# A fused decoder layer on one core: output weights staged elsewhere, start loads reordered, last mixing on VectorE, and a new order of all steps

## The reference

```python
x = x + attn(layernorm(x), wq, wk, wv, wo)           # (4, 512, 256), 16 heads, keys of 16, values of 64
x = x + xattn(ctx, ctx, layernorm(x), fm_w, fm_b, fc_w, fc_b)
x = x + ffn(layernorm(x), W_r, W_k, W_v, mu_r, mu_k)
# attn: softmax over the query axis of q.k / 4, times v, then the output projection
# xattn: features exp(z), exp(-z) of queries and of 64 context rows, softmax over the 64, then fc
# ffn: xr = prev + mu_r (x - prev), xk = prev + mu_k (x - prev);  out = sigmoid(xr W_r) * (relu(xk W_k)^2 W_v)
```

## Time and profile before

| | |
|---|---|
| median of 3 executions | 449.89 us (449.42 to 451.17) |
| the profiled execution | 449.9 us |
| its span | 448.1 us |
| instructions | 8243 |
| TensorE clock granted, mean | 1.00 |

### The profile page before, as it was taken

The page is one execution under the profiler, slowest core; times in us unless marked ns, Lnnn a source line. Parts: engine busy times, 40 slices in busy tenths (PEclk is TensorE's granted clock), DMA queues, the critical chain, the costliest instruction groups (busy, mean ns, idle before and its releaser), DMA issues.

```text
span 448.1 us, 8243 instructions
## 1 busy us (share of the span) xinstructions
PE 426.5 (95%) x2738; PEld 274.4 (61%) x2738; DVE 367.7 (82%) x668; ACT 300.9 (67%) x760; POOL 161.2 (36%) x206
## 2 busy tenths in 40 slices
PE   6999999999989999999999999999999999879896
PEld 4745454466545865566655785576555674467775
DVE  4688877798998887888999978798999888669762
ACT  3687988676796666666778566666787757529521
POOL 2163203117232513427052622427331533534442
PEclk9999999999999999999999999999999999999999
DMA  7668302435210015145103002642003100000001
GB/s 241 234 236 269 142 1 96 143 107 197 75 47 1 1 55 179 64 150 187 45 6 119 0 2 103 197 153 91 0 1 111 57 1 1 23 2 1 1 25 47
DMA packets 22561, 38.23 MB, mean 85 GB/s; under 512 B 2808, under 2 KB 7160, under 8 KB 22392
## 3 DMA queue, kind: packets, MB, share of 16 engines
q1 hardware_dynamic: 22520, 37.71, 24.6%
HBM read 23.02 MB, written 14.68 MB: 84 GB/s over the span
## 4 chain that ended last, share of the span: by engine, by line
PE 75%; DVE 9%; ACT 8%; issue 4%; DMA 1%; POOL 1%; SPq 0%; POOLq 0%; ACTq 0%; DVEq 0%
PE av_bank L909 22%; PE m_bank L841 9%; PE s_pair L895 8%; PE m_bank L845 6%; DVE nmax L1355 4%; ACT e_sb L1148 3%; PE m_bank L1045 3%; PE m_bank L961 2%; PE m_bank L1057 2%; PE m_bank L982 2%; PE m_bank L1117 2%; PE m_bank L1106 2%; PE m_bank L926 2%; PE m_bank L1073 2%; PE m_bank L945 1%
## 5 line engine op out<-in xcount | busy, mean ns | idle before, releaser
L1148 ACT ACTIVATE e_sb<-s_pair,nmax 128x512 f32<-128x512 f32 x256 | 174.1, 692 | 62.0 <-DVE nmax L1355 61.8
L1355 DVE TENSOR_REDUCE nmax<-s_pair 128x2 f32<-128x1024 f32 x128 | 152.4, 1213 | 21.5 <-PE s_pair L895 20.6
L909 PE MATMUL av_bank<-e_sb,v_sb 128*64 128x512 f32 x512 | 120.1, 602 | 1.0 <-POOL v_sb L1627 0.8
L1627 POOL TENSOR_TENSOR v_sb<-v_sb,rsum 128x256 f32<-128x256 f32 x64 | 39.7, 622 | 156.6 <-DVE rsum L1363 156.6
L909 PEld LDWEIGHTS av_bank<-e_sb,v_sb 128*64 128x64 f32 x512 | 32.6, 136 | 62.8 <-issue 53.2
L895 PE MATMUL s_pair<-q_st,k_st 64*128 64x512 f32 x256 | 49.9, 456 | 4.8 <-ACT e_sb L1148 4.8
L1148 ACT ACTIVATION_READ_ACCUMULATOR e_sb<-s_pair,nmax 128x1 f32 x256 | 53.6, 209 | 0.0
L895 PEld LDWEIGHTS s_pair<-q_st,k_st 64*128 64x128 f32 x256 | 21.3, 184 | 39.1 <-ACT e_sb L1148 25.2
L841 PE MATMUL m_bank<-wo_hi,ot_hi 128*128 128x256 f32 x128 | 36.4, 290 | 0.0
L845 PE MATMUL m_bank<-wo_lo,ot_hi 128*128 128x256 f32 x128 | 35.0, 279 | 0.0
L1654 POOL TENSOR_TENSOR sx<-sx,xrec 128x512 f32<-128x512 f32 x24 | 24.8, 1045 | 26.9 <-DVE xrec L1541 26.9
(11 more groups left out here) (186 smaller groups left out, 830.9 us busy)
## 6 DMA issues: line engine op xcount, KB each, us to landing
q_st<-q_parts SPq DMA_DIRECT2D x31, 256.0 KB, 3.8
k_st<-k_parts SPq DMA_DIRECT2D x31, 256.0 KB, 3.8
k_parts<-qkt_hi SPq DMA_DIRECT2D x7, 512.0 KB, 3.1
k_parts<-qkt_lo SPq DMA_DIRECT2D x7, 512.0 KB, 4.1
q_parts<-qkt_hi SPq DMA_DIRECT2D x8, 256.0 KB, 2.0
q_parts<-qkt_lo SPq DMA_DIRECT2D x8, 256.0 KB, 2.3
out<-x_sb SPq DMA_DIRECT2D x8, 256.0 KB, 2.2
x_sb<-in_x SPq DMA_DIRECT2D x3, 512.0 KB, 5.0
```

Source lines behind the costliest of these rows:

```text
L909: mm = pe.matmul(av_bank[n % AV_BANKS][64 * par:64 * par + 64, :], v_sb[:, m, 2 * p + par, :], e_sb[:, (4 * q + 2 * i + par) % E_RING, :], ...
L1148: act.activation(e_sb[:, g % E_RING, :], s_pair[k // 2][:, k % 2, :], ACT.Exp, bias=nmax[:, g % 8:g % 8 + 1], accum_out=esum[:, q % 4, k:k ...
L1355: dve.tensor_reduce(nmax[:, at:at + 2], s_pair[i][:, :, :], AX_X, ALU.max, negate=True)\
L1627: pool.tensor_tensor(v_sb[:, m:m + 2, 2 * p:2 * p + 2, :], v_sb[:, m:m + 2, 2 * p:2 * p + 2, :], rsum[:, q % 4, :].rearrange("p (m h) -> p ...
```

## The change

1. The output weights are staged in `sx`, the tile of the cross scores; the value projections lose their wait for them, and the first write of `sx` (`xs`, DVE) gains one.
2. SP loads the query/key weights second, right behind x; the output weights follow the value weights at once, and the feature loads move behind `ld 3`, the `fc` weights behind `ld 7` of sequence 0.
3. In `xs` and `pv` on PE the waits for what was done long ago come first; odd `xs` steps drop the wait for `z`.
4. The output projection of the last half-set of heads is split in two steps, `op` and `op_last`.
5. For sequence 3 `mix_r` is finished on DVE by two SCALAR_TENSOR_TENSOR instructions (`mix_rec`) instead of three on POOL.
6. All places are new. ACT at the start: `cut v1` from place 21 to 4, both `t1` before `cut first`; DVE: `t1 (0)` before `cut qk`, `qk (1, 0)` before the first `max`; POOL: `cut v1` from place 5 to 3. PE keeps the first twelve steps, then swaps `v (0, 2)` and `qk (1, 0)`. In the middle most steps move by a few places. Around attention step 22 `t2 (1)` goes four places up on PE, and on ACT `v`, `xs` and `pt` copies go behind the four `exp` of step 21; on ACT `t1 (0)` of sequence 1 goes behind `exp [5, 3]`. At the end: DVE's `fv 2 (0)` goes from before `ot_lo 31` to between `ln2_do (1)` and `t2 (1)`; POOL's `mix 2 (1)` goes behind both `ln2`; on PE `xs (1)` goes before `z (1)` and on ACT `z (1)` before `xs (0)`; the two `warm` steps after `fr 3 (0)` and the four after `fv 3 (0)`, and the one between the last `fk` and `fr`, are elsewhere: PE has `fr 3 (0)`, `t3 (1)`, `fv 3 (0)`, `fk 3 (1)`, `fr 3 (1)`, `fv 3 (1)` in a row, and seven `warm` steps behind them.

The lines of the diff outside the tables (of the tables a few stand for the rest):

```diff
-    ("cut", 0, ("v1",), dict(act=21, pool=5)),
+    ("cut", 0, ("v1",), dict(act=4, pool=3)),
-    ("load", 0, ("feat",), dict(sp=0)),
-    ("load", 0, ("o",), dict(sp=1)),
+    ("load", 0, ("feat",), dict(sp=8)),
+    ("load", 0, ("o",), dict(sp=0)),
...
-        wo_raw = v_sb[:, :, H // 2:, :].rearrange("p t h v -> p t (h v)")
+        wo_raw = sx
...
-                if before or unit[1] == B - 1:
+                if before or unit[1]:
                     eng.wait_ge(exp_ready, TILES)
...
+            sp.dma_start(wqk_raw, wqk).then_inc(wqk_in, 16)
             sp.dma_start(id_sb[:], ident).then_inc(id_in, 16)
             sp.dma_start(first_raw, wfirst).then_inc(first_in, 16)
-            sp.dma_start(wqk_raw, wqk).then_inc(wqk_in, 16)
...
-                for p in range(4):
-                    if p == 3:
-                        pe.wait_ge(ot_hi_ready, b * NP + 4 * hh + 4)
+                for p in range(3):
...
+                if (b, hh) != (B - 1, 1):
+                    op_last(b, hh, tt)
+            def op_last(b, hh, tt):
+                unit = ("op", b, (hh, tt))
+                pe.wait_ge(ot_hi_ready, b * NP + 4 * hh + 4)
...
             def xs(b, t):
+                if t == 0:
+                    pe.wait_ge(kblk_ready, b + 1)
                 for unit in units:
                     wait_bank(pe, unit)
-                for r in range(2):
-                    wait_emptied(pe, ("z", b, (t // 2, r)))
-                if t == 0:
-                    pe.wait_ge(kblk_ready, b + 1)
+                if t % 2 == 0:
+                    for r in range(2):
+                        wait_emptied(pe, ("z", b, (t // 2, r)))
...
             def fr(b, half):
-                pe.wait_ge(mixr_ready, 2 * b + half + 1)
+                if b == B - 1:
+                    pe.wait_ge(mixr_last, half + 1)
+                else:
+                    pe.wait_ge(mixr_ready, 2 * b + half + 1)
...
-                    if b == 0 and hh:
-                        act.wait_ge(cut_lo["o"], 1)
...
-                    if b == 0 and hh:
-                        dve.wait_ge(cut_lo["o"], 1)
...
                 link(dve.tensor_reduce(xmax[:, n % 4, :], src, AX_X, ALU.max, negate=True))
+                if n == 0:
+                    dve.wait_ge(cut_lo["o"], 1)
...
+            def mix_rec(b, half):
+                dve.wait_ge(mixk_ready, 2 * b + half + 1)
+                prev = xt3[:, :, half * HALF:(half + 1) * HALF]
+                for c in range(DC):
+                    ins = dve.scalar_tensor_tensor(out=mix_r[:, c, :], in0=mix_r[:, c, :], scalar=mu_sb[:, 0, c:c + 1],
+                                                   in1=prev[:, c, :], op0=ALU.mult, op1=ALU.add)
+                ins.then_inc(mixr_last, 1)
```

More of the change, by code:

```diff
@@ L130 @@
[L130 to L139, removed]
+    ("warm", 0, (3, 1), dict(pe=341)),
@@ L485 @@
[L485 to L486 removed]
+    dict(scores=14, weigh=21, max=(14, 15), exp=(13, 14, 15, 16), rsum=19, scale=4),
+    dict(scores=17, weigh=22, max=(17, 18), exp=(18, 19, 20, 21), rsum=21, scale=5, ot_hi=30, ot_lo=29),
+    dict(scores=20, weigh=28, max=(22, 23), exp=(23, 24, 25, 26), rsum=30, scale=7),
+    dict(scores=23, weigh=29, max=(26, 27), exp=(27, 28, 31, 32), rsum=31, scale=8, ot_hi=38, ot_lo=37),
@@ new lines @@
+    dict(scores=66, weigh=75, max=(87, 88), exp=(97, 98, 99, 100), rsum=96, scale=23),
+    dict(scores=69, weigh=80, max=(91, 93), exp=(103, 105, 106, 107), rsum=97, scale=26, ot_hi=120, ot_lo=110),
+    dict(scores=72, weigh=84, max=(98, 100), exp=(109, 110, 111, 112), rsum=107, scale=27),
+    dict(scores=76, weigh=85, max=(104, 105), exp=(116, 117, 118, 119), rsum=111, scale=28, ot_hi=127, ot_lo=121),
+    dict(scores=82, weigh=91, max=(112, 113), exp=(122, 124, 125, 126), rsum=119, scale=29),
@@ new lines @@
+    dict(scores=109, weigh=127, max=(151, 154), exp=(168, 170, 172, 173), rsum=166, scale=46),
+    dict(scores=116, weigh=128, max=(157, 159), exp=(176, 177, 180, 181), rsum=167, scale=47, ot_hi=195, ot_lo=177),
+    dict(scores=121, weigh=136, max=(163, 165), exp=(185, 186, 187, 188), rsum=179, scale=49),
+    dict(scores=126, weigh=137, max=(170, 171), exp=(190, 191, 192, 193), rsum=180, scale=50, ot_hi=205, ot_lo=185),
+    dict(scores=129, weigh=142, max=(175, 178), exp=(197, 198, 199, 201), rsum=186, scale=53),
@@ new lines @@
+    dict(scores=159, weigh=169, max=(213, 216), exp=(235, 236, 238, 239), rsum=221, scale=63),
+    dict(scores=163, weigh=173, max=(219, 222), exp=(243, 244, 247, 248), rsum=227, scale=66, ot_hi=260, ot_lo=236),
+    dict(scores=168, weigh=181, max=(226, 228), exp=(253, 255, 256, 257), rsum=232, scale=69),
+    dict(scores=174, weigh=182, max=(233, 234), exp=(263, 264, 265, 266), rsum=239, scale=70, ot_hi=277, ot_lo=249),
+    dict(scores=179, weigh=189, max=(238, 240), exp=(270, 271, 272, 273), rsum=250, scale=73),
@@ new lines @@
+    dict(scores=209, weigh=219, max=(280, 281), exp=(311, 313, 314, 315), rsum=290, scale=86),
+    dict(scores=213, weigh=220, max=(286, 287), exp=(317, 318, 319, 320), rsum=292, scale=87, ot_hi=327, ot_lo=297),
+    dict(scores=216, weigh=232, max=(291, 293), exp=(322, 323, 325, 326), rsum=299, scale=90),
+    dict(scores=221, weigh=234, max=(296, 300), exp=(328, 329, 330, 331), rsum=310, scale=91, ot_hi=346, ot_lo=316),
+    dict(scores=225, weigh=239, max=(303, 305), exp=(334, 335, 336, 339), rsum=315, scale=93),
@@ L487 @@
+    dict(scores=282, weigh=288, max=(378, 379), exp=(416, 417, 418, 419), rsum=382, scale=117, ot_hi=427, ot_lo=389),
+    dict(scores=286, weigh=291, max=(383, 384), exp=(422, 423, 424, 426), rsum=388, scale=119),
+    dict(scores=289, weigh=292, max=(386, 387), exp=(428, 429, 430, 431), rsum=390, scale=120, ot_hi=432, ot_lo=391),
 ]
```

704 lines of the change are left out of this document (347 added, 357 removed).

## The result

| | before | after |
|---|---|---|
| median of the executions | 449.65 us (449.18 to 451.17, 4) | 444.05 us (442.98 to 445.27, 4) |
| ratio, 95% interval | | 0.9872 [0.9847, 0.9896] |
| the profiled execution, its span | 449.9 us, 448.1 us | 445.27 us, 443.5 us |
| TensorE clock granted in it | 1.00 | 0.992 |

The change takes 1.3% off, 5.6 us by the medians.

The account below looks back on a forecast made before the run. It took PE, busy 426.5 of 448.1 us, as the bound, with an engine-to-engine chain at the start and after 380 us. Sum: 449.9 - 1.5 - 0.5 + 0.3 - 1.7 = 446.5 us, range 444.4 to 449.0.

Parts of the forecast that it names:

- I put two or three of them, +1.0: Middle: new waits made by the new order, two or three of 0.2 to 0.5 us each, costing +1.0 us.
- I take -1.5 there: Middle: gain from the two largest PE stalls, 0.86 and 1.24 us around 126 us, taken as -1.5 us.
- The start, -1.5: Start: earlier weights and first scores give -0.7, shorter `exp` chains -0.8; -1.5 us, bounds -2.4 and 0.
- The features and the staging: Feature loads moved behind `ld 3`, and output weights staged in `sx`: each claimed to cost 0.
- The middle, -0.5: PE's stalls after 48.08 us: -1.5 from stalls near 126, +1.0 for new waits; -0.5 us, bounds -3.0 and +2.0.
- Up to 416 us, +0.3: The end up to 416 us: ACT starts with `z (1)`, the same work 0.25 later; +0.3 us, bounds -0.3 and +1.0.
- the +0.6: Phase up to 416 us: its cost by the skill's rule, with `fv 2 (0)` waiting for POOL's bias addition; +0.6 us.
- The last microseconds, -1.7: Last half: `fk` starts earlier and `fr` right behind it, at 438.65 instead of 440.35; -1.7 us, bounds -1.0 and -1.9.
- The stalls mostly go: Rival on the middle: most PE stalls vanish, middle -2.5, total 444.5 us; chance 0.11.
- the order costs it: Rival: the new order costs in the middle what the start gains, +2.0 in place of -2.0; 448.8 us, chance 0.22.
- The clock's rival: Rival at the end: without `warm` steps after `fr 3 (0)`, PE's clock falls to half in pauses from 433.1; 451.7 us, chance 0.04.

Follow-up runs that it names:

- runs 4, 5, 6: 4: kernel before with new end, 450.54 us; 5: changed kernel with mixing on POOL, 446.59, or four warm back, 445.15; 6: changed kernel, old waits and staging, 444.44.
- the second kernel of run 5: The changed kernel with four `warm` steps put back between `fv 3 (0)` and the last `fk`; 445.15 us, 0.9893.

## Why the prediction was wrong

Its sum was -1.5, -0.5, +0.3, -1.7. The runs give -1.5, -3.0, +0.2, -1.7, together -6.0, and by the medians at full clock it is 449.19 - 443.32 = 5.9: **three of four terms held, and the failed step is the middle's**, "I put two or three of them, +1.0" together with "I take -1.5 there". Two more things moved the number. The sum started from the profiled 449.9, which is 0.7 above the 449.19 of full clock; some 0.3 of that is that its weights landed at 8.64, the latest of the five profiles of that load order (8.35 by the mean). And the half clock took 0.7 us of the gain back by the medians (444.05 against 443.32), which hid a part of the miss.

- *The start, -1.5.* Measured -1.5 alone, in part by luck, since two errors cancel. Weights at 6.81 to 7.68 (forecast 7.4), PE 3.7 us behind them (3.55), so PE's own start gains 0.2 by the means and not 0.45, and the first steps 1.2 and not the 1.05 left. Wrong in one detail: POOL did not hold `weigh 0` to 28.5, it began at 27.85. The features and the staging cost 0, as said.
- *The middle, -0.5.* Two errors of opposite kind, and the second decides. The stalls near 126 us gave less than the 1.5 assumed: 0.86 + 1.24 = 2.10 became 0.27 + 0.69 + 0.22 = 1.18, so 0.9 (0.6 with steps 20 to 23 alone). But the +1.0 had even the wrong sign: new waits came, 1.50 us further back, and they replaced 2.12 us of old ones, which the prediction had left standing; of the waits at 65 and 78 us (0.68) 0.15 was left; PE's busy time for the same matmuls fell by 0.55 (not shown to be waiting, though likely); and 0.55 came at step 63, which the prediction had counted with nothing. Its premise, that a move in the middle is worth only the idle time that it touches, missed the last two. An order that moves nearly every step by a few places was priced as if it fixed one spot and spoilt others; it had fixed many small ones.
- *Up to 416 us, +0.3.* In profiles at full clock the stretch from the second scores of step 63 to `pv 3 (0)` took 31.3 us before and 31.5 in all three profiles of the new end (`warm` step back, four `warm` steps back, identity first): +0.2. Against the two other profiles of the old end at full clock there, the start's and that of steps 20 to 23 (31.0), it is +0.5, so the size is good to a few tenths only. The reading of the second `fv 2 (0)` instruction was right: it took 1.27 us and not 0.69 and ended 0.55 behind POOL's bias addition (395.06 to 396.33). That agrees closely with the rule of the Trainium skill, "SBUF — State Buffer", section "Who interferes with whom", that the later of such a pair waits for the whole of the other; a wait for all of it would have ended it 0.69 behind. The phase as a whole lost 0.2 to 0.5, less than the +0.6 that the prediction made of the rule.
- *The last microseconds, -1.7.* 7.77 to 6.11 is -1.66; `fk` 0.14 us behind `mix_k`, `fr` released by nothing.
- *The rivals.* "The stalls mostly go", middle -2.5 and 444.5 us at a chance of 0.11, is the one that came; "the order costs it" at twice that chance had nothing for it but that stalls exist, and its 448.8 doesn't follow from its terms (449.9 - 1.5 + 2.0 + 0.3 - 1.7 = 449.0). The clock's rival had the wrong place: from 420 us to PE's last matmul the clock is 1.00 in every profile. But the argument against it, "PE stood idle for 2.23 us ... and the granted clock stayed at 1.00", falls: in three other profiles of the old load order a pause of 1.83 to 1.99 us at the same place was followed by 0.50. One execution that keeps its clock shows nothing of the next. The rule of the Trainium skill, "TensorE: Matmul & The Clock Gate", section "Part 1: The HAM clock gate", that idle stretches bring the half clock, was the better guide: these profiles agree with it in kind, as each fall stands behind pauses (1.83 to 1.99 us here, the four below), though the same pauses don't always bring one.

In the changed kernel the clock took back part of the gain. Its profile has 0.50 from 394.5 to 401.3 us, behind pauses of 0.58, 0.78, 0.30 and 0.55 us, and the stretch from the second scores of step 63 to `pv 3 (0)` took 33.85 us in it and not 31.5:

```profile
391.64 0.63 PE L930 MATMUL s_pair<-id_sb,xn 128*128 128x128 f32 x4 [0.58 <-DVE xn L715]
393.04 0.39 PE L1040 MATMUL s_pair<-xt_hi,fm_hi 64*128 64x256 f32 x2 [0.78 <-ACT xt_hi L1263]
394.08 0.51 PE L1040 MATMUL s_pair<-xt_lo,fm_hi 64*128 64x256 f32 x4 [0.30 <-DVE xt_lo L1489]
395.13 1.09 PE L930 MATMUL s_pair<-id_sb,xn 128*128 128x128 f32 x4 [0.55 <-DVE xn L715]
```

The five kernels with the new end and without the `warm` step there (runs 4, 5, 6 and the changed kernel) were at full clock in 8 of 34 executions, the two with it in 9 of 11. The new end alone has the old start, whose pause near 11 us brings falls too; without it the first count is 7 of 22. The step in its old place costs nothing: up to `pv 3 (0)` it is 31.51 us with it there, and 31.50 in the second kernel of run 5, which has it where the changed kernel does. By the medians of all executions the kernels with it took 443.72 and 443.94 us against 444.05, and their intervals overlap. That they are faster isn't shown. That the step keeps the clock up is likely, not settled: a mean below 1.00 doesn't tell where the clock fell, and some of these kernels differ elsewhere too. Nor does the step prevent every fall. The kernel of steps 8 to 34 has the old end with the step in its place and the pauses of before there (0.96, 0.34, 0.30 and 0.54 us between 395.5 and 399.9; before 0.96, 0.34, 0.30 and 0.55), and its profile shows 0.50 from 401 to 404 us, where the profile of before kept 1.00.

## What to carry over

Price a rewritten order by all the waits that it touches, the short ones too, and compare the busy time of the same matmuls too; a fear that "a new order makes waits of its own" needs a row before it gets a number. Two edits that shorten the same chain can hide each other: the removed `warm` steps gave nothing without the mixing on DVE, and the mixing half of the gain without them, so test them alone and as a pair. A part kernel should hold nothing but its part; where it holds more, show that the rest counts for nothing. Filler work in front of real work is judged over many executions by the clock they were granted, not by one profile, and filler moved to the end must not outlast the real work there.

## What was not expected of the hardware

- The granted clock fell to 0.50 behind four pauses of only 0.3 to 0.8 us (391.1 to 395.1 us in the changed kernel), and behind a single one of 1.83 to 1.99 us at the start in three profiles; with 2.23 us at that place the profile of before kept 1.00, and with the changed kernel's four pauses (0.51, 0.78, 0.29 and 0.54 us) that of the kernel with four `warm` steps back kept it too. An execution of the kernel before at a mean of 0.996 took 449.8 to 451.2 us, against 449.2 at full clock.
- The landing of the same 512 KB varied between profiles of one load order by 0.9 us (6.81 to 7.68), with nothing in it changed. That is more than half of what the start gained.
